# Logistic weights, a rounded third head and DRAM copies in the output pass of a four-layer graph network kernel

## The reference

```python
hW = h @ W                                   # for each of 3 heads
hp = (node_adj > 0) @ hW;  hm = (node_adj < 0) @ hW
e_plus  = leaky_relu(concat([hp, hm]) @ a)   # one score for each node
e_minus = leaky_relu(concat([hm, hp]) @ a)
att = where(edge_adj > 0, e_plus[None, :], NEG_INF)
att = where(edge_adj < 0, e_minus[None, :], att)
support += (softmax(att, axis=1) * edge_adj) @ hW / 3
...
node_output = gru_cell(support, h, node_Wih, node_Whh, node_bih, node_bhh)
return de * edge_output + dn * node_output   # gru: r, z = sigmoid; n = tanh; (1-z)*n + z*h
```

## Time and profile before

| | us |
|---|---|
| median of three runs (lowest, highest) | 2103.26 (2102.48, 2103.84) |
| the profiled execution, its own time | 2101.93 |
| its span, first to last instruction | 2100.1 |
| PE busy over the span | 1875.6 (89%) |
| DVE busy | 1663.2 (79%) |
| ACT busy | 1469.0 (70%) |

### The profile page before, as it was taken

One profiled execution on the slowest core, in us unless ns is written; L12 is line 12 of the kernel. 1 busy time (PEld: TensorE's weight loads), 2 busy tenths in 40 slices (PEclk: granted clock), 3 DMA queues, 4 the chain that ended last, 5 costly groups with the idle time before them and its releaser, 6 DMA issues.

```text
span 2100.1 us, 22007 instructions
## 1 busy us (share of the span) xinstructions
PE 1875.6 (89%) x7997; PEld 1195.3 (57%) x7997; DVE 1663.2 (79%) x2462; ACT 1469.0 (70%) x1453; POOL 13.4 (1%) x15
## 2 busy tenths in 40 slices
PE   2335999789998989989999989899999999999997
PEld 1223888578877989965555556444444444444443
DVE  4658989698877888887878762698889888988985
ACT  3445666456668999988777631597878878887873
POOL 0000000000010000000000000000000000000000
PEclk9999999899999999999999999999999999999999
DMA  9999899588885777669999698443232323423220
GB/s 389 429 428 378 324 343 344 192 292 317 318 314 185 250 247 248 249 229 360 350 336 357 247 338 288 136 135 130 86 110 105 112 104 115 132 97 117 105 75 11
DMA packets 81563, 489.51 MB, mean 233 GB/s; under 512 B 8449, under 2 KB 12546, under 8 KB 36402
## 3 DMA queue, kind: packets, MB, share of 16 engines
q1 hardware_dynamic: 77138, 485.94, 62.8%
q10 hardware_dynamic: 4320, 2.20, 0.4%
HBM read 452.36 MB, written 35.75 MB: 232 GB/s over the span
## 4 chain that ended last, share of the span: by engine, by line
PE 63%; DVE 16%; ACT 10%; DMA 7%; issue 3%; SPq 0%; DVEq 0%; ACTq 0%
PE bank L1749 26%; DMA ring<-in_adj_rows 7%; PE bank L1551 5%; PE bank L1711 5%; PE bank L1553 5%; PE bank L1552 5%; ACT work L630 4%; DVE work L1395 3%; ACT work L625 3%; PE bank L1625 2%; DVE a_lo L982 2%; DVE reg L1395 1%; PE bank L1654 1%; PE bank L1630 1%; PE bank L1631 1%
## 5 line engine op out<-in xcount | busy, mean ns | idle before, releaser
L1749 PE MATMUL bank<-work,reg 128*128 128x512 f32 x960 | 422.5, 595 | 17.3 <-DVE ring L1344 11.4
L1395 DVE TENSOR_TENSOR work<-work,ring 128x1536 f32<-128x1536 f32 x160 | 280.3, 1752 | 68.0 <-ACT work L803 67.1
L1749 PEld LDWEIGHTS bank<-work,reg 128*128 128x128 f32 x960 | 181.8, 191 | 246.2 <-issue 220.2
L982 DVE TENSOR_TENSOR a_lo<-ring,a_hi 128x2048 fp32r<-128x2048 f32 x128 | 292.5, 2301 | 31.0 <-ACT a_hi L574 30.1
L574 ACT ACTIVATE a_hi<-ring 128x2048 fp32r<-128x2048 f32 x128 | 244.2, 1912 | 76.3 <-PE bank L1553 76.3
L1585 PE MATMUL bank<-reg,ring 128*128 128x129 f32 x2048 | 242.6, 281 | 27.6 <-DVE ring L1096 27.4
L1585 PEld LDWEIGHTS bank<-reg,ring 128*128 128x128 f32 x2048 | 238.0, 197 | 31.5 <-DVE ring L1096 20.7
L803 ACT ACTIVATE work<-work 128x1536 f32<-128x1536 f32 x160 | 235.3, 1471 | 26.1 <-DVE work L1373 26.1
L1749 PE MATMUL bank<-reg 128*128 128x512 f32 x576 | 252.4, 592 | 0.0
L1551 PE MATMUL bank<-a_hi,s_hi 128*128 128x512 f32 x512 | 206.8, 404 | 21.2 <-DVE a_lo L982 21.2
L1553 PE MATMUL bank<-a_hi,s_lo 128*128 128x512 f32 x512 | 201.6, 394 | 0.0
(11 more groups left out here) (235 smaller groups left out, 2649.4 us busy)
## 6 DMA issues: line engine op xcount, KB each, us to landing
ring<-in_adj_units SPq DMA_DIRECT2D x320, 1024.0 KB, 4.9
ring<-in_adj_rows SPq DMA_DIRECT2D x32, 2048.0 KB, 17.0
ring<-masks SPq DMA_DIRECT2D x64, 512.0 KB, 4.6
...
```

Of the source, the lines that this page charges most:

```text
L982: dve.tensor_tensor(a_lo[:, ring_at(p, g)], ring[:, ring_at(p, g)], a_hi[:, (g % 4) * UNIT:(g % 4 + 1) * UNIT].bitcast(F32), ALU.subtract) ...
L1395: dve.tensor_tensor(tv, tv, spread(ring[:, ring_at("out", g, q * W, W)], HEADS, 1), ALU.mult).then_inc(s_y, 1)
L1749: last = pe.matmul(bank[1 + k][:, :], h, tiles(c * T + t)[:, k * W:(k + 1) * W], start=t == 0, stop=t == T - 1)
```

## The change

Five things change, all in the output pass and its surroundings.

1. **Weights.** `first_clamps`, `clamps` and the Exp over 1536 are gone. ACT makes each head's weights with one Sigmoid over 128x512, `sigmoid(e - guard)` (`weights`), two tiles ahead. The guards are 20 higher (`MARGIN`), so that the logistic function equals the exponential to rounding, and the denominators carry exp(-20). If the matrix has negative entries (a flag made on the chip), DVE first works out arguments (`arguments`); with this input it is not called.
2. **Third head.** For tiles 0 to 29 of a chunk the third head's f32 matmul becomes three fp32r matmuls (`third_tile`). ACT makes the rounded high part (`third_high`, one Copy over 128x512), DVE the rest (`third_low`, one subtraction over 128x512). There are three buffers for high parts (`PLACES`) and seven tiles (`TILES`, was 8). Tiles 30 and 31 stay in f32.
3. **Order at the end of a chunk.** Tiles 30 and 31 are multiplied head by head, each head's sum is counted by itself (`s_head`), and `take_chunk` and `heads` wait head by head.
4. **The end of the program.** The last chunk's gates have their hidden halves multiplied early, and the reset gate's Tanh goes first.
5. **DRAM copies.** SP stores `reg2` and `x` to DRAM (2 MB each) during the norm pass, before mask loads 20 and 28, and loads 256 KB of each for every chunk.

The diff, cut to what matters (buffers, ACT's and SP's part):

```diff
+
+            b = n % TILES
+            if b < 5:
+                return plain[:, b * THREE:(b + 1) * THREE]
+            return reg[:, 0:THREE] if b == 5 else tail[:, 13 * W:13 * W + THREE]
...
+        def cut_index(n):
+
+            return (n // T) * CUT + n % T
+
+        def tile_low(n):
+
+            return tile_of(n, a_hi, s_lo, spare_r)[:, LAST * W:HEADS * W]
+
+        def tile_high(n):
+
+            first = THREE + cut_index(n) % PLACES * W
+            return s_lo[:, first:first + W]
...
+            def load_chunk(c):
+
+                if c > 1:
+                    sp.wait_ge(s_res["out"], c - 1)
+                else:
+                    sp.wait_ge(s_xs, 16)
+                    sp.wait_ge(s_hs, 16)
+                sp.dma_start(x_chunk, xs_d[:, (c - 1) * W:c * W]).then_inc(s_xload, 16)
+                sp.dma_start(h_chunk, hs_d[:, (c - 1) * W:c * W]).then_inc(s_hload, 16)
+
             for n in range(MASKS, C * G):
+                if n == 20:
+                    sp.wait_ge(s_gv["edge"], C * CELL_STEPS)
+                    sp.dma_start(hs_d, reg2[:, :]).then_inc(s_hs, 16)
+                if n == 28:
+                    sp.wait_ge(s_res["edge"], C)
+                    sp.dma_start(xs_d, x[:, :]).then_inc(s_xs, 16)
                 load_masks(n)
             load_guards(0)
             load_guards(1)
             for n in range(RING_OUT, C * G):
                 load("out", n)
+                if n > G and n % G == 2:
+                    load_chunk(n // G)
                 if n % G == 6:
                     c = n // G
                     load_dens(c)
                     if c and c + 1 < C:
                         load_guards(c + 1)
+            load_chunk(C)
 
 
         @block.gpsimd
...
 
-            def first_clamps(n):
+            def weights(n):
 
                 c, t = n // T, n % T
                 if t == 0:
                     act.wait_ge(*guards_loaded(c))
-                if n >= GROUPS:
-                    act.wait_ge(s_used, n + 1 - GROUPS)
-                elif n >= 5:
+                if n >= TILES:
+                    act.wait_ge(*tile_used(n - TILES))
+                elif n >= AHEAD:
                     act.wait_ge(s_mm["norm"], G * C)
-                for k in range(on_act(t)):
-                    last = act.activation(tiles(n)[:, k * W:(k + 1) * W], guard(c, k), ACT.Relu,
-                                          bias=(ne0, ne1)[k][:, t:t + 1])
-                last.then_inc(s_relu, 1)
-
-            first_clamps(0)
+                    act.wait_ge(s_hs, 16)
+                act.wait_ge(s_arg, n + 1)
+                for k in range(HEADS):
+                    last = act.activation(tiles(n)[:, k * W:(k + 1) * W], guard(c, k), ACT.Sigmoid,
+                                          bias=e6[:, t * SCORES + k:t * SCORES + k + 1], scale=-1.0)
+                last.then_inc(s_exp, 1)
+
+            def third_high(n):
+
+                i = cut_index(n)
+                if i >= PLACES:
+                    act.wait_ge(*tile_used(i - PLACES + 2 * ((i - PLACES) // CUT)))
+                act.wait_ge(s_y, n + 1)
+                act.activation(tile_high(n), tiles(n)[:, LAST * W:HEADS * W], ACT.Copy).then_inc(s_yhi, 1)
+
+            for n in range(AHEAD):
+                weights(n)
             for c in range(C):
                 for t in range(T):
...
-                    if n + 1 < C * T:
-                        first_clamps(n + 1)
-                    act.wait_ge(s_clamp, n + 1)
-                    act.wait_ge(s_relu, n + 1)
-                    act.activation(tiles(n), tiles(n), ACT.Exp, scale=-1.0).then_inc(s_exp, 1)
+                    if n + AHEAD < C * T:
+                        weights(n + AHEAD)
+                    if t < CUT:
+                        third_high(n)
             keep_edge_support(C)
-            gates("out", C)
+            act.wait_ge(s_lastg, 1)
+            act.wait_ge(s_gv["out"], (C - 1) * CELL_STEPS)
+            act.activation(n_temps[1], bank[5][:, :], ACT.Tanh, bias=gb[:, 4:5], scale=0.5).then_inc(s_lastr, 1)
+            act.wait_ge(s_gm["out"], C)
+            act.activation(n_temps[2], bank[6][:, :], ACT.Tanh, bias=gb[:, 5:6], scale=0.5).then_inc(s_ga["out"], 1)
             candidate("out", C)
             store(C)
             act.wait_ge(s_store, 16 * C)
```

DVE's part:

```diff
                 s.link(dve.tensor_tensor(g_at(6), g_at(2), g_at(3), ALU.add))
-                s.inc(dve.tensor_tensor(g_at(4), g_at(2), g_at(6), ALU.subtract))
+                s.link(dve.tensor_tensor(g_at(4), g_at(2), g_at(6), ALU.subtract))
+                s.inc(dve.tensor_scalar(g_at(4), g_at(4), MARGIN, None, ALU.add))
...
                 s.link(dve.tensor_tensor(g_at(0), g_at(1), g_at(5), ALU.mult))
-                s.link(dve.tensor_scalar(g_at(0), g_at(0), 1.0e-30, None, ALU.max))
+                s.link(dve.tensor_scalar(g_at(0), g_at(0), 1.0e-28, math.exp(-MARGIN), ALU.max, ALU.mult))
...
             def take_chunk(c):
 
-                dve.wait_ge(s_used, c * T)
                 dve.wait_ge(s_dens, 16 * c)
                 if c > 1:
                     dve.wait_ge(s_es, c - 1)
                 for k in range(HEADS):
+                    dve.wait_ge(s_head, HEADS * (c - 1) + k + 1)
                     dve.tensor_tensor(nk[:, k * W:(k + 1) * W], bank[1 + k][:, :],
                                       rden[:, k * W:(k + 1) * W], ALU.mult).then_inc(s_nk, 1)
 
...
+
+                dve.wait_ge(s_yhi, cut_index(n) + 1)
+                dve.tensor_tensor(tile_low(n), tiles(n)[:, LAST * W:HEADS * W], tile_high(n).bitcast(F32),
+                                  ALU.subtract).then_inc(s_ylo, 1)
...
+                    dve.sem_inc(s_arg, C * T)
...
-                        if n + AHEAD < C * T:
-                            clamps(n + AHEAD, negatives)
...
                         tv = tiles(n).rearrange("p (k i) -> p k i", k=HEADS)
                         dve.tensor_tensor(tv, tv, spread(ring[:, ring_at("out", g, q * W, W)], HEADS, 1),
                                           ALU.mult).then_inc(s_y, 1)
+                        if 0 < t <= CUT:
+                            third_low(n - 1)
```

PE's part:

```diff
+            def third_tile(c, t):
+
+                n, h = c * T + t, slice(t * P, (t + 1) * P)
+                acc, high, low = bank[1 + LAST][:, :], tile_high(n), tile_low(n)
+                pe.matmul(acc, h_hi[:, h], high, start=t == 0, stop=False)
+                pe.matmul(acc, h_hi[:, h], low, start=False, stop=False)
+                return pe.matmul(acc, h_lo[:, h], high, start=False, stop=False)
...
-                    for q in range(Q):
+                    for q in range(Q if g < G - 1 else Q - 2):
                         t = g * Q + q
-                        h = reg1[:, t * P:(t + 1) * P]
+                        pe.wait_ge(s_y, c * T + (t + 1))
                         for k in range(HEADS):
                             if t == 0 and c:
                                 pe.wait_ge(s_nk, HEADS * (c - 1) + k + 1)
...
-                            if k == 0:
-                                pe.wait_ge(s_y, c * T + (t + 1))
-                            last = pe.matmul(bank[1 + k][:, :], h, tiles(c * T + t)[:, k * W:(k + 1) * W],
-                                             start=t == 0, stop=t == T - 1)
+                            if k == LAST:
+                                pe.wait_ge(s_ylo, cut_index(c * T + t) + 1)
+                                last = third_tile(c, t)
+                            else:
+                                head_tile(c, t, k)
                         last.then_inc(s_used, 1)
...
+                pe.wait_ge(s_y, (c + 1) * T)
+                for k in range(HEADS):
+                    last = head_tile(c, T - 2, k)
+                    if k == HEADS - 1:
+                        last.then_inc(s_used, 1)
+                    head_tile(c, T - 1, k).then_inc(s_head, 1)
+
+            src, h = n_temps[0], h_chunk
+            pe.wait_ge(s_hload, 16 * C)
+            pe.wait_ge(s_res["out"], C - 1)
+            pe.matmul(bank[5][:, :], gate_w(1, 1, 0), h, start=True, stop=False)
             heads(C)
-            gates("out", C)
+            pe.matmul(bank[6][:, :], gate_w(1, 1, 1), h, start=True, stop=False)
+            pe.matmul(bank[7][:, :], gate_w(1, 1, 2), h, start=True, stop=True)
+            pe.wait_ge(s_src["out"], C)
+            pe.matmul(bank[5][:, :], gate_w(1, 0, 0), src, start=False, stop=True).then_inc(s_lastg, 1)
+            pe.matmul(bank[4][:, :], gate_w(1, 0, 2), src, start=True, stop=True).then_inc(s_lastg, 1)
+            pe.matmul(bank[6][:, :], gate_w(1, 0, 1), src, start=False, stop=True).then_inc(s_gm["out"], 1)
             turn_cells("out", C)
 
```

137 lines of the change are left out of this document (79 added, 58 removed).

## The result

| | before | after |
|---|---|---|
| median (lowest to highest), us | 2102.87 (2102.29 to 2103.84), 4 runs | 2068.56 (2067.95 to 2069.2), 4 runs |
| ratio after/before | | 0.9836 [0.9819, 0.9853] |
| span of the profiled execution | 2100.1 | 2067.4 |

A forecast was written before the change was run, and what follows sets the result against it. PE was taken to set the pace of the output pass, with DVE and ACT close behind. Terms -40.8 + 7.0 + 3.2 + 5.5 + 1.5 - 5.3 = -28.9 gave 2074 us from the runs' median; range 2066 to 2084, chance 0.48.

The forecast's parts named there:

- PE's work, 240 tiles: Third head of 30 tiles in 8 chunks: three fp32r matmuls save 0.17 us a tile, type changes free; -40.8 us.
- lead used up within chunks 1 to 7: DVE's lead runs out by tile 21, so PE waits 1.0 us in each of chunks 1 to 7; +7.0 us.
- diagonal, chunks 4 to 7: The diagonal's four small DVE operations at t = 4c, not made good in chunks 4 to 7; 4 x 0.8 = +3.2 us.
- the seven chunk ends: PE waits 1.9 us for `take_chunk` behind DVE's next-chunk work, about the 2.0 of before; counted as nothing.
- chunk 0: No lead yet: `norm_nodes_in` +3.1, 1.3 left of two table loads, `guard_rows` 0.4, the end 0.7; together +5.5 us.
- norm pass, and what lies before it: Two 2.1 MB stores compete with mask loads while DMA is full: between nothing and 11.2, taken as +1.5 us.
- the end: From PE's last tile to `cell_in`: 7.1 us instead of 12.4, one gate product covering the last `nk`; -5.3 us.
- the walk through the chunk: DVE's lead over PE: 5.0 by tile 12, 3.8 after t = 17, 1.9 after `cell_in`, about 0.1 at t = 21.
- The rival that the lead suffices: Boundary waits go too if DVE or ACT are faster or lead remains: 2043 to 2066 us, chance 0.20.
- Whatever holds up ACT or DVE is made good by only 0.05 us a tile: Output pass rates: with engines at 2.41, 2.35 and 2.27 us a tile, delays are regained at 0.05 a tile.
- the 0.3 at tile 25: PE's wait at t = 25: `result` costs DVE 1.2 us, 0.4 is regained and PE's transposes give 0.4.
- the 0.7 at tile 31: Chunk's end: PE, without lead, waits for product 31, 1.67 behind the last low part; 0.7 us.

The follow-up runs named there:

- the last experiment but one: Changed kernel with `take_chunk` behind tile 1, stores at mask loads 40 and 52, norm_nodes_in at tile 20, last norm chunk's remaining work in chunk 1: 2051.26 us, ratio 0.975.
- two buffers: Changed kernel with two buffers for the high parts instead of three (`PLACES` = 2): 2084.11 us, ratio 0.9908 to the kernel before.
- tile by tile: Changed kernel with tiles 30 and 31 multiplied tile by tile again and one count for all three sums: 2069.07 us, ratio 0.9831.
- the old end: Changed kernel with the end of the program as before (heads, all six gate products, both Tanh, then `cell_in`): 2070.37 us, ratio 0.9839.
- the later stores: Changed kernel with the two 2 MB stores before mask loads 40 and 52 instead of 20 and 28: 2064.8 us, ratio 0.981.
- the repetition: The changed kernel once more, unchanged, beside two others on the same chip: 2067.64 us, ratio 0.9826 to the kernel before.

## Why the prediction was right, point by point

The terms of its sum, and what the spans give for each:

| term | forecast | measured |
|---|---|---|
| PE's work, 240 tiles | -40.8 | -40.4 |
| lead used up within chunks 1 to 7 | +7.0 | +1.1 |
| diagonal, chunks 4 to 7 | +3.2 | +2.8 |
| the seven chunk ends | 0 | -1.7 |
| chunk 0 | +5.5 | +6.4 |
| slow clock at the start of chunk 1 | - | +1.7 |
| norm pass, and what lies before it | +1.5 | +2.0, +0.7 |
| the end | -5.3 | -5.3 |
| sum | -28.9 | -32.7 (span: -32.7) |

How they are worked out. A tile costs PE 2.575 before and 2.407 now, 0.168 less. From its first record to the end of its last one PE needs 90.67 for a chunk before and 85.78 for chunks 2 and 3 now, 4.89 less, where 30 tiles give 5.05: the 0.16 between is all that can be put down to the lead, 1.1 in seven chunks. Chunk 4 takes 85.85, chunks 5, 6 and 7 take 86.70: the diagonal, nothing in chunk 4 and 0.9 in each of the others. Chunk 1 takes 87.48, 1.7 more than chunk 2: the slow clock. From a chunk's last record to the next chunk's first it is 1.65 instead of 1.94, at six chunk ends; the first one is in the row of chunk 0. Chunk 0, from PE's start to its next, is 86.3 before and 87.6 now with 5.1 less to do: 6.4. The norm pass took 121.2 instead of 119.2 and began 0.7 later, before anything that the change touches in this view.

**Right.** PE sets the pace, each tile is 0.17 shorter, and changing type twice in a tile costs nothing (1682.37 to 1692.00). ACT at 2.36 and DVE at 2.27 a tile are as priced. DVE's queue decides the chunk's end, and PE loses 1.65 there, where 1.9 was forecast. The lead is bounded by the three high parts; the walk through the chunk holds to tile 21: 5.0 forecast and 5.0 seen at tile 16, 3.8 and 3.9 at tile 17, 1.9 and 2.1 at tile 18, 0.1 and 0.5 at tile 21 (seen: from the low part's end to the moment when PE has its turn). The end of the program came to the tenth. The rival that the lead suffices is half true: within the chunks it does, at their ends it does not, and `take_chunk` comes every 87.4, just under the 88 to 89 that I had named.

**The step that failed** is the term "+7.0", and in it the sentence "Whatever holds up ACT or DVE is made good by only 0.05 us a tile". At tile 25 the low part ends at 1681.74 and PE's turn for it is at 1682.37 less 0.23 = 1682.14, 0.4 ahead; at tile 29 it ends at 1690.82 and the turn is 1691.77, 0.95 ahead. That is 0.14 a tile: DVE's own 2.27 against 2.41. The slower ACT does not hold it back, because a hold-up of DVE alone lets ACT run ahead. The high part of tile 26 is ready at 1681.86 and taken at 1683.32, 1.46 later; that of tile 29 at 1688.94, taken at 1690.13, 1.19 later. ACT's 2.36 lags DVE's 2.27 by 0.09 a tile, and this stock pays for it. In chunk 0, where ACT is the late one and has no stock, 0.05 is right, as the last experiment but one shows. I had used one rate for both. With 0.14 the 0.3 at tile 25 and the 0.7 at tile 31 do not come. The term for the diagonal is near in sum but not in its parts: at tile 16 of chunk 4 the lead is still full, 5.0, and hides it; at tiles 20, 24 and 28 of the next chunks it costs 0.9 each.

**Luck.** The lead, the diagonal and the chunk ends came out 8.0 below the forecast. Chunk 0, the slow clock at the start of chunk 1, which was not in the sum at all, the norm pass with what lies before it, and PE's work came out 4.2 above. That the sum is 3.8 off and not 8 is because these errors have opposite signs.

**Chunk 0** was sized about right, 6.4 for 5.5, for partly wrong reasons. I had added up what PE would wait for one thing after the other. In fact DVE and ACT hardly wait for PE in this chunk, and their own chain sets its length. In the six executions whose DVE and ACT have the same work in the same order here (the changed kernel twice, two buffers, tile by tile, the old end, the later stores) the low part of tile 6 ends 21.8 us after PE's first tile and that of tile 29 78.4 to 78.5 after it, and the chunk takes 87.57 to 87.60, while PE's wait at tile 6 goes from 2.04 to 3.44 us. The wait is the shorter, the longer TensorE was at 1.2 GHz at the start of the pass, so neither that slow stretch nor the one behind tile 6 costs these kernels time: a later wait takes it up. `norm_nodes_in` holds DVE from 1362.59 to 1367.28, as priced. The table loads cost 2.5, where I had 1.3, because ACT does not make up for them before the chunk ends. At `guard_rows` DVE waits 1.0 for ACT's high part of tile 20, where I had 0.4.

**Open.** Why the clock falls behind some waits and not behind others was not tried; the length of the wait does not decide it. At the start of chunk 1 six executions have the same wait of 2.0: in four a slow stretch follows, in two (the later stores, the repetition) none. At tile 6 of chunk 0 it followed waits of 1.98 to 2.75 in six executions and did not follow waits of 3.29 to 3.44 in three. That the norm pass begins 0.7 later is within what this start does from run to run (1219.3 to 1222.2 in all profiles).
